# A decoder layer on one core: the triangular solve in staggered 32-row pieces, with the work around it reordered

## The reference, cut to what matters

```
x = x + delta_net(layernorm(x))          # 4 heads of 64, chunks of 32 tokens
x = x + cross_attention(layernorm(x), context of 64 tokens, masks)   # 16 heads of 16
x = x + moe(layernorm(x))                # 8 experts, the best 2 per token, and a shared one
```

```
A    = strictly lower part of kb @ k.T
Tinv = inverse of (eye + A)
u, w = Tinv @ v, Tinv @ kb
# then, from chunk to chunk:
u = u - w @ S;  o = q @ S + lower(q @ k.T) @ u;  S = S + k.T @ u
```

## Time and profile before

| | us |
|---|---|
| median of 3 runs (lowest to highest) | 1239.55 (1238.06 to 1245.83) |
| the profiled execution, its time | 1235.7 |
| its span in the trace | 1233.6 |
| TensorE busy (share of the span) | 1073.1 (87%) |
| VectorE busy | 861.6 (70%) |
| POOL busy | 618.9 (50%) |
| ScalarE busy | 528.2 (43%) |
| mean granted TensorE clock | 0.96 |

### The profile page before, as it was taken

How to read it: one execution, slowest core, us unless ns; L and a number is a source line. 1 busy time by engine, 2 the same in 40 slices (tenths; PEclk the granted TensorE clock), 3 DMA queues, 4 the chain that set the end, 5 groups by cost and what they waited for, 6 DMA issues and landing times.

```text
span 1233.6 us, 24158 instructions
## 1 busy us (share of the span) xinstructions
PE 1073.1 (87%) x8466; PEld 822.0 (67%) x8466; DVE 861.6 (70%) x2236; ACT 528.2 (43%) x968; POOL 618.9 (50%) x1030
## 2 busy tenths in 40 slices
PE   4899969697799999899999999999989888977892
PEld 2555648576676767777776686686677666766782
DVE  3899968754777777876867777777778465555477
ACT  3877845215024424413522522432441245734661
POOL 7887636174038437536645734833750233344552
PEclk9999989798899999999999999999999889998996
DMA  8366440701001601601230150130110342323488
GB/s 198 102 191 186 145 151 4 259 24 69 18 2 61 203 2 44 189 27 44 101 121 25 55 179 2 60 126 1 61 65 6 150 171 91 96 78 101 145 281 305
DMA packets 86789, 127.56 MB, mean 103 GB/s; under 512 B 28304, under 2 KB 62608, under 8 KB 84496
## 3 DMA queue, kind: packets, MB, share of 16 engines
q1 hardware_dynamic: 79472, 106.30, 27.9%
q0 software_dynamic: 7200, 19.74, 4.4%
HBM read 66.47 MB, written 59.55 MB: 102 GB/s over the span
## 4 chain that ended last, share of the span: by engine, by line
PE 43%; POOL 16%; DVE 7%; issue 6%; ACT 4%; another core or an unknown queue 2%; DMA 1%; SPq 1%; ACTq 0%; POOLq 0%; DVEq 0%
PE bank L696 7%; POOL arena L1463 6%; POOL arena L1465 6%; PE bank L508 2%; PE bank L666 2%; PE bank L762 2%; PE bank L548 2%; PE bank L752 2%; PE bank L914 2%; POOL orn L1480 2%; PE bank L562 2%; PE bank L675 2%; ACT arena L1083 2%; PE bank L574 2%
## 5 line engine op out<-in xcount | busy, mean ns | idle before, releaser
L988 ACT ACTIVATE arena<-bank 128x512 f32<-128x512 f32 (+2 forms) x358 | 186.8, 541 | 453.1 <-PE bank L574 122.8
L1527 POOL DMA_INDIRECT results<-arena x78 | 76.7, 984 | 100.3 <-DVE arena L2142 72.0
L1589 DVE SCALAR_TENSOR_TENSOR arena<-arena,param 128x512 f32<-128x512 f32 x144 | 108.0, 767 | 12.6 <-ACT arena L1011 9.1
L1463 POOL TENSOR_TENSOR arena<-arena 128x126 f32<-128x126 f32 (+22 forms) x217 | 91.5, 422 | 38.0 <-DVE arena L1685 22.4
L1447 POOL COPY arena<-arena 32x128 f32<-32x128 f32 x128 | 51.8, 404 | 94.9 <-DVE arena L1675 89.0
L696 PEld LDWEIGHTS bank<-arena 128*128 128x128 f32 x768 | 93.0, 200 | 5.3 <-issue 4.3
L1465 POOL TENSOR_TENSOR arena<-arena 128x126 f32<-128x126 f32 (+22 forms) x217 | 87.2, 402 | 17.0
L696 PE MATMUL bank<-arena 128*128 128x128 f32 x768 | 93.9, 283 | 0.0
L1399 POOL DMA_INDIRECT slots_x<-arena x64 | 63.1, 986 | 49.2 <-DVE arena L1881 31.9
L914 PE MATMUL bank<-arena 128*128 128x128 f32 x624 | 86.6, 284 | 0.4 <-ACT arena L1260 0.2
L1961 DVE TENSOR_TENSOR arena<-arena,bank 128x512 f32<-128x512 f32 x96 | 62.0, 683 | 27.2 <-PE bank L696 18.6
(11 more groups left out here) (273 smaller groups left out, 2733.7 us busy)
## 6 DMA issues: line engine op xcount, KB each, us to landing
arena<-slots_x SPq DMA_DIRECT2D x78, 129.0 KB
slots_x<-rows_of_no_token SPq DMA_DIRECT2D x8, 1161.0 KB
xt<-x_in SPq DMA_DIRECT2D x16, 512.0 KB, 6.2
kq_T<-kq SPq DMA_DIRECT2D x8, 1024.0 KB, 4.5
kq<-kq_T SPq DMA_DIRECT2D x8, 1024.0 KB
arena<-results SPq DMA_DIRECT2D x32, 256.0 KB
arena<-ffn_in SPq DMA_DIRECT2D x7, 768.0 KB, 4.1
vT<-v_T SPq DMA_DIRECT2D x8, 514.0 KB
```

What stands on the lines that cost most here:

```text
L988: free(act.activation(out_, in_, func, **kw), name)
L1463: own.link(pool.tensor_tensor(tmp, rows32[:, m0:, k].unsqueeze(2).broadcast_to([P, nm, k]), units[:, 0:k, k].unsqueeze(1).broadcast_to([P, ...
L1527: pool.indirect_dma_start(results[:, :], bass.IndirectOffsetOnAxis(ap=dest[:, n % YS:n % YS + 1], axis=0), ys[:, n % YS, :], None).then_in ...
L1589: ins = V.scalar_tensor_tensor(cv[:, k % 4, :], pre[:, j, d:d + GT], param[:, at + d:at + d + 1], cv[:, k % 4, :], ALU.mult, ALU.add)
```

## The change

The solve no longer steps through all rows of all tiles. Quarter q of tile t is computed only when the quarters above it are right, and only its 32 rows. The pairs (t, q) are taken along diagonals, six of them, with up to three pairs of different tiles and different quarters in each. TensorE's output is a strip of 32 partitions in bank t, and VectorE updates the 32 rows of UW in place. ScalarE writes the first product to UW, and Y is read by that product alone.

```
+DIAGONALS = tuple(tuple((t, s + 1 - t) for t in reversed(range(T)) if 1 <= s + 1 - t < NQ) for s in range(T + NQ - 2))
 # TensorE
+                def solve(s):
+                    mine = DIAGONALS[s]
+                    for t, q in mine:
+                        open_bank(pe, f"solve{t}{q}.{i}", t)
+                    for h in range(H):
+                        for t, q in mine:
+                            qq = slice(QB * q, QB * q + QB)
+                            last = mm(banks[t][qq, h * P:(h + 1) * P], NT[:, t * H + h, qq], UW[:, t * H + h, :],
+                                      start=True, stop=True)
+                            if h == H - 1:
+                                full(last, f"solve{t}{q}.{i}")
 # VectorE
+                def solve(s):
+                    for t, q in DIAGONALS[s]:
+                        n = f"solve{t}{q}.{i}"
+                        o = filled(dve, n)
+                        if q == 1:
+                            drained(dve, f"solve{t}0.{i}")
+                        rr, tt = slice(QB * q, QB * q + QB), slice(t * H, (t + 1) * H)
+                        free(V.scalar_tensor_tensor(UW[rr, tt, :], UW[rr, tt, :], 1.0,
+                                                    o[rr, :].rearrange("p (h c) -> p h c", h=H),
+                                                    ALU.mult, ALU.subtract), n)
```

The order on TensorE in a body with cross attention (`effects(t)` is the old `wa` loop's inside):

```
                     context()                     # before: after the products
                 if i != 1:
                     front_squares(i, (2, 3, 0, 1) if i else range(T))      # banks
                     front_product(i, range(T - 1) if x else range(T))
...
+                    solve(0)
+                    if i != 1:
+                        front_product(i, (T - 1,))
+                    rows()
+                    solve(1)
+                    queries(0)
+                    solve(2)
+                    queries(1)
+                    solve(3)
+                    if i >= 2:
+                        positions(i - 2, 6)           # before: between squares and products
+                    masked_scores(0)
+                    if ahead:
+                        front_values(i + 1, 0)
+                    solve(4)
+                    effects(0)
+                    if ahead:
+                        front_values(i + 1, 1)
+                    solve(5)
+                    effects(1)
+                    effects(2)
+                    turned_scores(0)
+                    if ahead:
+                        front_values(i + 1, 2)
+                    masked_scores(1)
+                    values(0)
+                    effects(3)
+                    if ahead:
+                        front_values(i + 1, 3)
+                    turned_scores(1)
+                    values_turned(0)
+                    if ahead:
+                        front_gram(i + 1, 0)
+                    values(1)
+                    masked_scores(2)
+                    values_turned(1)
```

and on VectorE, behind `masks` and the short filter:

```
+                    context()                     # before: behind rows2 and slots
                     rows2()
...
+                    solve(0)
+                    anykey()
+                    solve(1)
+                    queries(0)
+                    solve(2)
+                    queries(1)
+                    solve(3)
+                    scores(0, (0,))
+                    solve(4)
+                    scores(0, (1,))
+                    effects(0)
+                    solve(5)
+                    effects(1)
+                    effects(2)
+                    if i >= 2:
+                        slots(i - 2)              # before: behind rows2, ahead of the solve
+                    scores(1)
+                    effects(3)
+                    values(0)
+                    if ahead:
+                        front_gram(i + 1, 0)
```

In body 0 both engines take `front_gram(1, t)` and `solve(t)` in turn, then effects and the last two diagonals. The other parts:

```
 # ScalarE, front_blocks
-                for r in range(NQ):
+                for r in range(NQ if i < 2 else NQ // 2):
 # VectorE, behind front_compact
+            def front_lower_blocks(i):
+                dve.wait_ge(sem("compact_ready"), i + 1)
+                for r in range(NQ // 2, NQ):
+                    rr = slice(QB * r, QB * r + QB)
+                    last = V.tensor_copy(Tf[rr, :, rr], Tc[rr, :, :].rearrange("p i h -> p h i"))
+                done(last, "lower_blocks_ready")
 # VectorE, end of the body
                 if x:
                     late_added()
-                    chosen(i - 1)
...
                     free(V.tensor_tensor(dst, dst, o[:, :].rearrange("p (t d) -> p t d", t=2), ALU.add), n)
+                if x:
+                    chosen(i - 1)
 # ScalarE
                 if i != 1:
                     front_squares(i, range(T))
+                    if i == 0:
+                        act.wait_ge(sem("long_ready"), CK * NG)
                     front_product(i)
 # POOL, front_rows: Y is free once the products are drained
-                        drained(pool, f"solve{t}{NQ - 1}.{i - 1}")
+                        drained(pool, f"solve{t}0.{i - 1}")
 # SP
                 if i + 1 < NG:
-                    if i:
-                        load_kq(i + 1)
                     load_v(i + 1)
                 if i:
                     load_late(i - 1)
+                if i + 2 < NG:
+                    load_kq(i + 2)
```

More of the change, by code:

```diff
@@ L688, in body, with effects @@
                      routing) = x
[L690 to L699, removed]
-                    context()
[L701 to L722, removed]
+                    context()
+                if i != 1:
+                    front_squares(i, (2, 3, 0, 1) if i else range(T))
+                    front_product(i, range(T - 1) if x else range(T))
+                def solve(s):
[9 more added lines that the diff above has]
+                                full(last, f"solve{t}{q}.{i}")
+                def effects(t):
                     drained(pe, f"solve{t}{NQ - 1}.{i}")
@@ L1087, in cross, with context @@
                 b, g = divmod(i, G)
-                def rows():
+                def context():
                     if g == 0:
@@ L1130, in late @@
                         evac(late_g[i][e], o[:, :], n, ACT.Silu)
-                return rows, probs, values, routing, router, late
+                return context, rows, probs, values, routing, router, late
             def front_squares(i, ts):
@@ L1281, in steps @@
                     at_step[0] += 1
-            rows, probs, values, routing, router, late = cross(NG - 1)
+            _, rows, probs, values, routing, router, late = cross(NG - 1)
             steps(5)
@@ L1993, in body @@
                     free(last, n)
[L1994 to L1995 removed]
+                if x:
+                    solve(0)
[6 more added lines that the diff above has]
+                    scores(0, (0,))
+                    solve(4)
+                    scores(0, (1,))
+                    effects(0)
+                    solve(5)
+                    effects(1)
+                    effects(2)
+                    if i >= 2:
+                        slots(i - 2)
+                    scores(1)
+                    effects(3)
+                    values(0)
+                    if ahead:
+                        front_gram(i + 1, 0)
+                else:
+                    filled(dve, f"N{T - 1}.{i}")
+                    for t in range(T):
+                        front_gram(1, t)
+                        solve(t)
+                    effects(0)
+                    solve(4)
+                    effects(1)
+                    solve(5)
+                    front_units(1)
+                    for t in range(2, T):
+                        effects(t)
                 if x:
                     scores(2)
[L1998 to L1999 removed]
                     values(1)
```

105 lines of the change are left out of this document (37 added, 68 removed).

## The result

The changed kernel takes 1268.85 us (1267.38 to 1273.55, four runs) against 1242.23 (1238.06 to 1245.83) of the kernel before beside it: ratio 1.0235, 95% interval 1.0203 to 1.0268, **slower by 2.4%**. Forecast were 1219 and a range of 1204 to 1240. The profiled execution has a span of 1266.4 us, 32.8 over the 1233.6 of before, and a mean granted clock of 0.94 against 0.96.

What follows compares the result with a forecast made beforehand. TensorE's work was taken to bound the first part of each body, with the POOL chain level within about 2 us. Body savings and block waits less end losses gave 19.1 us: 1216.6 to 1220.5, said 1219, range 1204 to 1240.

Steps and rivals of the forecast that it cites:

- slots, scatter and POOL: Slots end 8.4 us ahead of `gm`; POOL's scatters and copies fit its 10.7 us idle time, slack 1 us, cost nothing.
- the walk: Step-by-step timing from squares to `gm`: 37.5 us in even bodies (2.9 saved), 40.2 in odd ones (2.0 saved).
- B: Rival: strips writing separate PSUM banks don't overlap on TensorE, 5.35 us more in seven bodies, 37 us: 1256 us; chance 0.07.
- C: Rival: POOL late from late `slots` or slower scatters, 1 us a body in five bodies, 1255 us at 8 late; chance 0.10.
- A: Rival: each diagonal waits for VectorE half a us more than walked, 21 us over seven bodies, about 1239 us; chance 0.20.
- E: Rival: short waits bring TensorE stretches at 1.2 GHz, not 2.4, 1.3 us each; inside the forecast, no chance of its own.
- The solve on TensorE: Six diagonals of 32-row strips replace three steps of 10.7 us a body: 7.0 us with switching, 3.7 less.
- On VectorE: Solve's twelve updates stay twelve, at 0.75 us instead of 0.69: +0.7 us, with six hand-overs instead of three.
- Blocks: VectorE takes two of ScalarE's four block copies: 2.1 us off the chain, four waits of 1.41 gone, 5.6 us.
- Ends: Body 0 loses 0.8 us, body 1 saves 1.6, body 7 saves 1.9; tail positions come 1.9 later.
- The sum: Savings of all bodies and block waits, less 0.8 and 1.9 us at the ends: 19.1 us in total.

Runs made afterwards that it cites:

- early_one_at_a_time: Changed kernel with positions matmul and slots back at their old early place, each scatter of the first six groups waiting for the last to land: 1215.64 us, ratio 0.9793.
- before_slots_late: Kernel before, old four-pass solve kept, with only positions matmul and slots moved late, so the scatter starts some 29 us into a body: 1303.88 us, ratio 1.0496.
- after_one_at_a_time: Changed kernel, slots and scatter left late, each scatter of the first six groups waiting for the one before to land: 1277.34 us, ratio 1.0295.
- before_blocks: Kernel before with only the lower two of the four block copies moved to VectorE: 1241.86 us, ratio 1.0008.
- early_twice: Changed kernel with positions and slots early, each scatter of the first five groups issued a second time into an unread table: 1310.47 us, ratio 1.0543.
- the small ones: Changed kernel, positions and slots early, first five groups' scatters issued again into an unread table with 8 numbers a row, not 258: 1298.58 us, ratio 1.046.
- early_pairs: Changed kernel with positions and slots early, scatters going out two together, GpSimd waiting for both before the next two: 1219.15 us, ratio 0.9822.

## Why the prediction was wrong, point by point

- **The step that failed** is the one that the prediction priced with "it was idle 10.7 us there, which is the cover" and "Slack: 1 us, so cost nothing": slots, scatter and POOL. It asked whether POOL had the time, and POOL had it: its first solve step comes 17.7 us after `gm` (675.56), as before. It did not ask what the scatter does to others while its packets move. Moved from a stretch with slack into one where TensorE, ScalarE and VectorE hand on every microsecond, it cost 8.9 us in body 4 against the walk, and 48 us over bodies 2 to 7 against the same kernel with the scatters one by one. Against early_one_at_a_time TensorE is idle 5.5 us more there (7.6 and 2.1) and busy 3.4 more (38.8 and 35.4), most of it in the matmuls behind the stall (L509, L590, L594 and L563 took 2.08, 1.08, 1.11 and 2.08 us, not 1.13, 0.65, 0.62 and 1.13); the granted clock fell from 2.4 to 1.2 GHz at 647.0, while TensorE stood idle behind its last matmuls of 645.1, and rose again at 657.2. Shown by before_slots_late (the move alone, +62 us), by early_one_at_a_time (the stalls away, 37.5 us) and by after_one_at_a_time (36.8 us in the changed order itself). The sign was to be had: "remote" stood in VectorE's rows of before, during the scatter, on a kernel of one core.
- **The rivals.** The time lies above the dearest of them (B, 1256 us); none had this mechanism. C had the right part of the change and the wrong mechanism: POOL is late only in after_one_at_a_time, not in the kernel after. B, strips that don't overlap, is refuted (24 instructions in 1.0 us, in three banks); the rule of the Trainium skill, TensorE: Matmul & The Clock Gate, Part 3, by which weight loads overlap only across row groups, does not hold for these strips, which share all rows. A is out: with the updates on time the hand-over costs no more than walked. E, the clock, came as a consequence of the stall: in body 4 of early_one_at_a_time it stays at 2.4 GHz.
- **The solve on TensorE**: 1.0 us a diagonal including the switching in, 6.0 us and the switching out, against the 7.0 forecast; the product behind the first diagonal takes 1.09 us to the next instruction. **On VectorE** an update of 32 rows takes 0.69 us, the old one's price, not 0.75.
- **The walk**: 37.5 us forecast for an even body, 37.0 to 37.5 in early_one_at_a_time, and 36.6 to 37.0 in after_one_at_a_time, whose order is the one walked. The 40.2 of an odd body holds the context, and so counts from its start, about 1.8 us ahead of the squares: from there bodies 3, 5 and 7 of early_one_at_a_time take 40.9, 40.2 and 40.6.
- **Blocks**: no wait for them, as said, and the reason "late next is TensorE itself" held only with edits that I had not tied to it: in before_blocks, without the new order of the squares' banks and `chosen` behind the adds, the gain is 0 us.
- **Ends**: the tail's wait for the positions is 1.79 us, forecast 1.9. The other 5 us of the longer tail of after I can't place; early_one_at_a_time is only 1.1 us longer there than before.
- **The sum** of 19.1 us comes out in a kernel without the disturbance, though one with its slots early: early_one_at_a_time's span is 20.2 us below before's. By parts: 2.8 saved up to the squares of body 2 (forecast 1.6 + 1.4 - 0.8 = 2.2), 18.5 from there to the last `gm` (8.7 + 4.0 + 1.9 + 4.2 = 18.8), 1.1 lost in the tail (1.9). By the medians it is 26 us (1242.0 and 1215.6), as the profiled execution of before (1235.7) is quicker than all its other runs. In the order that was forecast no run reached this: its slots are late, and the scatters then hold up either TensorE's updates or POOL.

What stays open is why a row of outstanding scatters holds up TensorE's semaphore updates and not VectorE's. The runs say when (several outstanding, whatever the bytes of the second ones), not through what. The ends of matmuls are modelled in the profile, so it could also be that the results themselves are late and the updates with them; TensorE went on starting matmuls until 644.62 us, with updates outstanding since 641.74, but no run parts the two.

## What to carry to other kernels

When a step is moved, ask not only whether its engine has time at the new place, but who runs beside it there: an indirect scatter that was free beside work with slack made a change that is worth 2% with the stalls away lose 2.4%, beside a tight chain. A wait that ends by "remote" or an unknown queue on one core is a clue worth following before a prediction is made. In a kernel like this one, try indirect DMAs one or two at a time where the issuing engine has the room, and leave them in a row where urgent work stands behind them on that engine.

## What the runs showed of the hardware

- While a row of indirect scatters is outstanding, semaphore updates of TensorE come late: up to 8.2 us beside a row of eight (after, bodies 2 to 6) and 12.7 beside sixteen (early_twice; 13.7 with the small ones); VectorE's own came after 0.01 us in the same stretch. With one outstanding none was more than 0.8 us late in bodies 2 to 6 of early_one_at_a_time, with two 1.3 in early_pairs. Pairs took 3.5 us more than single ones in all, with intervals that overlap; how many it takes was not measured beyond that.
- One scatter of 128 rows takes 0.96 us of POOL's time and lands 1.8 to 2.3 us later when it goes out by itself behind the loads; second scatters with 8 numbers a row instead of 258 disturb as much (311.1 and 311.5 us from squares to `gm`).
- Weight loads and matmuls of three tiles of 32 columns that share all 128 rows and write three banks run fully side by side: 8, 16 and 24 instructions each in 1.0 us.
